# A two-layer gated cross-attention and feed-forward kernel: attention and FFN of a layer as one program with fixed, overlapping SBUF places

## The chip, the cores and the metric

One NeuronCore of a Trainium2 chip runs the whole kernel. The metric is the device time of one execution in microseconds (us). The kernel before takes 2742.32 us (median of 3 runs, 2741.12 to 2743.13).

## The reference, cut to what matters

Two layers work on `x`, 4096 rows (2 batches of 2048) of 512 values, against a context of 154 keys per batch. All is float32.

```
x = x + tanh(g_xattn[0]) * xattn0(layernorm(x), ctx)          # 16 heads of 32, softmax over 154 keys
x = x + tanh(g_ffn[0])   * (relu(layernorm(x) @ W1 + b1) @ W2 + b2)
x = x + tanh(g_xattn[1]) * xattn1(ctx, layernorm(x), mask)    # q, k, v are also layer-normalised
h = float2fix(layernorm(x) @ w1 + b1)                         # rounded to multiples of 1/256
h = float2fix(pwlin_gelu_basic(h))                            # 33-point piecewise linear GELU
x = x + tanh(g_ffn[1])   * float2fix(h @ w2 + b2)
```

W1 is 512 x 2048 and W2 is 2048 x 512.

## The kernel before

Every float32 product is made of three fp32r products, hi·hi, hi·lo and lo·hi (`hi_lo_matmul`, L56 is its matmul), so every weight and every left or right side is split into a hi part (ScalarE copies it as fp32r) and a lo part (the rest, by VectorE or GpSimd).

A layer is three programs, one after another, each with its own SBUF tiles, semaphores and an all-engine barrier at its end (`Named.end`): `context_phase` makes keys and values; `attention_phase` runs over 8 chunks of 512 rows; `ffn_phase` runs over the same 8 chunks. Between them the stream goes through DRAM. In the traces `l_ctx`, `l_att` and `l_ffn` tell them apart, for both layers alike.

Attention. The order of each engine is written out by hand. TensorE in chunk `it`: the transposes of the next chunk's rows (`xT_front`), the row maxima (`neg_front`, L836), the scores of the 26 tail keys, then per group of heads `scores_main` and `values_of`, with the next chunk's query products (`q_front`, four products of 12 matmuls) set between them as filler; `recips` (transposes of the reciprocal sums of the chunk before, L936), then `max_of` of the next chunk interleaved with `y_back` of the chunk before (48 matmuls of the output projection, L56 into `l_att_bank`). In the last chunk (7) nothing follows, so filler and `max_of` fall away. Then comes the drain: `sums_front(7)` (L919), `recips(7)`, `y_back(7)`. `y_back` has two PSUM banks; its rows are taken out by VectorE (L694), which needs the residual tile `xg` with its bias (`add_gate_bias`, GpSimd, L441), and `xg` is loaded only once the chunk before is stored (SP: `store`, then `load_residual`).

FFN. The hidden side is 16 tiles `m` of 128. Tile `u = 16*it + m` takes a first product (12 matmuls into `hid`), an activation, a split, and a second product (12 matmuls into the four accumulators `acc`) three tiles later (`LAG`). In layer 0 the activation is `relu_hi` on ScalarE and `relu_lo` on VectorE. In layer 1 it is a loop of three engines: VectorE `round_hidden` (L1277), ScalarE `gelu_ends` (three operations), GpSimd `slope_of` (L1136), VectorE `gelu` (L1284, L1289, L1293: three operations with two SBUF inputs each), ScalarE `rounded_hi` (L1202, L1207), VectorE `rounded_lo` (L1299). VectorE's order in tile `u` is `round_hidden(u)`, `rounded_lo(u-2)`, `gelu(u-1)`; ScalarE's is `gelu_ends(u)`, `rounded_hi(u-1)`.

The FFN weights stay in SBUF as hi and lo. They are brought in during chunk 0, tile by tile, through one staging buffer: two DMAs of 256 KB (SP: `weights(m)`, which waits until the lo parts of the tile before are made), two copies on ScalarE (`weights_hi`, L1213), two subtractions on GpSimd (`weights_lo`, L1124). `first_product` of chunk 0 waits for them tile by tile.

## Time and profile before

| what | value |
|---|---|
| median of 3 runs | 2742.32 us |
| the profiled execution, own time | 2744.99 us |
| its span, first to last instruction | 2743.2 us |
| TensorE matmul busy | 2480.5 us, 90% |
| VectorE, ScalarE, GpSimd busy | 53%, 39%, 18% |
| mean granted TensorE clock | 0.955 |
| DMA | 140.92 MB, mean 51 GB/s |
| layer 0 attention / FFN, TensorE's first to last matmul | 67.4 to 536.0 / 561.6 to 1282.3 us |
| layer 1 attention / FFN, TensorE's first to last matmul | 1364.4 to 1929.6 / 1950.5 to 2730.8 us |

The page cuts the span into 40 slices of 68.6 us; each digit is a busy share in tenths. A timeline row gives start, duration, engine, line, operation, output<-inputs, shape and count, and in square brackets the engine's idle time before it with its releaser. Rows of a group of instructions give busy us and the mean ns of one.

### The profile page before, as it was taken

The numbers are of one execution on the slowest core, as the hardware profiler recorded it, in microseconds if no ns is written. First come the engines' busy times: TensorE is split into PE (matmuls) and PEld (weight loads), VectorE is DVE, ScalarE is ACT, GpSimd is POOL, SyncE is SP. The second block draws the span as 40 slices with busy tenths as digits, with TensorE's granted clock in tenths as the row PEclk, the third lists the DMA queues.
The fourth block names the chain that finished last, engine by engine and source line by source line (L and its number), as shares of the span: only waits on it lengthen the run. The fifth ranks groups of instructions, "written<-read, shape, count | busy, mean of one in ns | idle before, by whom it ended". The sixth has DMA issues, their size and how long they took to land. (4 is left out here: it accounts for less than half of the span.)

```text
span 2743.2 us, 32089 instructions
## 1 busy us (share of the span) xinstructions
PE 2480.5 (90%) x12840; PEld 1860.6 (68%) x12864; DVE 1463.2 (53%) x2222; ACT 1078.3 (39%) x1734; POOL 505.4 (18%) x411
## 2 busy tenths in 40 slices
PE   4899999779999999996489999999579999999997
PEld 3557667458888888885355566665467788778776
DVE  4455565232222222211655665553488888888887
ACT  3233443243222222222223333332355666666564
POOL 1011211252000000001101111111462222222221
PEclk8799999889999999998699999999799999999999
DMA  3002111232001100102210111111321010101100
GB/s 129 31 16 81 59 47 47 86 114 81 16 31 46 46 27 20 47 31 75 95 41 28 59 59 59 59 44 62 100 82 53 16 46 32 47 16 34 44 16 31
DMA packets 87941, 140.92 MB, mean 51 GB/s; under 512 B 4848, under 2 KB 27760, under 8 KB 87792
## 3 DMA queue, kind: packets, MB, share of 16 engines
q1 hardware_dynamic: 87792, 138.87, 14.9%
q8 instruction: 102, 1.67, 0.2%
q14 instruction: 47, 0.39, 0.0%
HBM read 105.30 MB, written 33.55 MB: 51 GB/s over the span
## 5 line engine op out<-in xcount | busy, mean ns | idle before, releaser
L56 PE MATMUL l_ffn_hid<-l_ffn_xT_hi,l_ffn_w_hi 128*128 128x512 f32 x1024 | 406.0, 397 | 29.3 <-POOL l_ffn_w_lo L1124 29.3
L56 PE MATMUL l_ffn_acc<-l_ffn_w_hi,l_ffn_h_hi 128*128 128x512 f32 x1024 | 402.6, 393 | 18.1 <-DVE l_ffn_h_lo L1299 18.1
L56 PE MATMUL l_ffn_hid<-l_ffn_xT_hi,l_ffn_w_lo 128*128 128x512 f32 x1024 | 402.0, 393 | 0.0
L56 PE MATMUL l_ffn_hid<-l_ffn_xT_lo,l_ffn_w_hi 128*128 128x512 f32 x1024 | 401.9, 392 | 0.0
L56 PE MATMUL l_ffn_acc<-l_ffn_w_lo,l_ffn_h_hi 128*128 128x512 f32 x1024 | 399.5, 390 | 0.0
L56 PE MATMUL l_ffn_acc<-l_ffn_w_hi,l_ffn_h_lo 128*128 128x512 f32 x1024 | 399.2, 390 | 0.0
L1269 DVE TENSOR_TENSOR l_ffn_h_lo<-l_ffn_full,l_ffn_h_hi 128x512 fp32r<-128x512 f32 x128 | 88.6, 692 | 501.0 <-ACT l_ffn_h_hi L1181 501.0
L1136 POOL TENSOR_TENSOR l_ffn_at_next<-l_ffn_at_next,l_ffn_at_grid 128x512 f32<-128x512 f32 x128 | 187.5, 1465 | 491.7 <-ACT l_ffn_at_next L1197 491.6
L1176 ACT ACTIVATE l_ffn_full<-l_ffn_hid,l_ffn_b 128x512 f32<-128x512 f32 x128 | 88.2, 689 | 447.8 <-PE l_ffn_hid L56 447.8
L56 PEld LDWEIGHTS l_ffn_hid<-l_ffn_xT_hi,l_ffn_w_hi 128*128 128x128 f32 x1024 | 194.5, 190 | 76.0 <-POOL l_ffn_w_lo L1124 36.4
L56 PEld LDWEIGHTS l_ffn_acc<-l_ffn_w_hi,l_ffn_h_hi 128*128 128x128 f32 x1024 | 192.7, 188 | 65.0 <-DVE l_ffn_h_lo L1299 25.9
L56 PEld LDWEIGHTS l_ffn_hid<-l_ffn_xT_hi,l_ffn_w_lo 128*128 128x128 f32 x1024 | 194.2, 190 | 41.1
L56 PEld LDWEIGHTS l_ffn_hid<-l_ffn_xT_lo,l_ffn_w_hi 128*128 128x128 f32 x1024 | 194.9, 190 | 39.7
L667 DVE TENSOR_REDUCE l_att_maxes<-l_att_score 128x4 f32<-128x616 f32 x256 | 199.2, 797 | 41.1 <-PE l_att_score L826 39.2
L56 PEld LDWEIGHTS l_ffn_acc<-l_ffn_w_hi,l_ffn_h_lo 128*128 128x128 f32 x1024 | 192.8, 188 | 40.5
L56 PEld LDWEIGHTS l_ffn_acc<-l_ffn_w_lo,l_ffn_h_hi 128*128 128x128 f32 x1024 | 192.8, 188 | 39.1
L526 ACT ACTIVATE l_att_p_main<-l_att_score 128x512 f32<-128x512 f32 x256 | 132.2, 604 | 160.1 <-PE l_att_score L875 160.1
L826 PE MATMUL l_att_score<-l_k_bd,l_att_qT_hi 128*128 128x308 f32 x512 | 155.1, 385 | 11.7 <-DVE l_att_maxes L667 11.6
L1202 ACT ACTIVATE l_ffn_at_grid<-l_ffn_at_grid,l_ffn_grid_bias 128x512 f32<-128x512 f32 x128 | 92.7, 724 | 166.0 <-DVE l_ffn_at_grid L1293 166.0
L1293 DVE SCALAR_TENSOR_TENSOR l_ffn_at_grid<-l_ffn_at_next,l_ffn_at_grid 128x512 f32<-128x512 f32 x128 | 153.6, 1200 | 4.4
L488 ACT ACTIVATE l_att_xT_hi<-l_att_bank 128x512 fp32r<-128x512 f32 x64 | 36.7, 597 | 288.8 <-PE l_att_bank L780 288.8
L450 POOL COPY l_att_r_wide<-l_att_rs 128x512 f32<-128x512 f32 x64 | 37.4, 614 | 598.3 <-DVE l_att_rs L687 508.8
(191 smaller groups left out, 4309.3 us busy)
## 6 DMA issues: line engine op xcount, KB each, us to landing
stream<-l_att_xg SPq DMA_DIRECT2D x16, 1024.0 KB, 4.3
l_ffn_x_in<-stream SPq DMA_DIRECT2D x16, 1024.0 KB, 5.5
l_ffn_stage<-in_l_w SPq DMA_DIRECT2D x64, 256.0 KB, 2.8
l_ffn_xg<-stream SPq DMA_DIRECT2D x16, 1024.0 KB, 5.5
l_att_x_in<-in_x SPq DMA_DIRECT2D x8, 1024.0 KB, 6.5
l_att_xg<-in_x SPq DMA_DIRECT2D x8, 1024.0 KB, 5.3
stream<-l_ffn_xg SPq DMA_DIRECT2D x8, 1024.0 KB, 4.3
l_att_x_in<-stream SPq DMA_DIRECT2D x8, 1024.0 KB, 6.7
```

Of the source, the lines that this page charges most:

```text
L56: done = nc.tensor.matmul(out, lhs[a], rhs[b], start=first and n == 0, stop=last and n == len(passes) - 1)
L450: nc.gpsimd.tensor_copy(r_wide[:, t % RB, :, :].rearrange("p q (j d) -> p (q j) d", j=GH), rs[:, t, :, :].rearrange("p q j -> p (q j)").un ...
L488: nc.scalar.activation(xT[0][:, k, :], bank[k % 2][:, :], ACT.Copy)\
L526: nc.scalar.activation(p_main[:, t % 2, j, :], score[:, j, :], ACT.Exp)\
L667: nc.vector.tensor_reduce(to, heads, AX.X, ALU.max).then_inc(max_done, 1)
L826: done = nc.tensor.matmul(to, qT[it % QB][0][:, t, q * P:(q + 1) * P], keys.bd[:, b, t, 2 * a:2 * a + 2, :], start=not masked, stop=True)
L1136: nc.gpsimd.tensor_tensor(at_next[:, u % 2, :], at_next[:, u % 2, :], at_grid[:, u % AB, :], ALU.subtract).then_inc(slope, 1)
L1176: nc.scalar.activation(full[:, u % 2, :], hid[u % 2][:, :], ACT.Relu, bias=b1[:, u % MT:u % MT + 1]).then_inc(h_full, 1)
L1202: nc.scalar.activation(at_grid[:, u % AB, :], at_grid[:, u % AB, :], ACT.Identity, bias=grid_bias[:, 3:4]).then_inc(rounded, 1)
L1269: nc.vector.tensor_tensor(h[1][:, u % HB, :], full[:, u % 2, :], h[0][:, u % HB, :].bitcast(F32), ALU.subtract)\
L1293: nc.vector.scalar_tensor_tensor(at_grid[:, u % AB, :], at_next[:, s, :], -4.0, at_grid[:, u % AB, :], ALU.mult, ALU.add)\
```

## The change

`attention_phase` and `ffn_phase` become one `layer_phase`: one block, no barrier between them. All large tiles have fixed byte offsets (`Place.at`) in one arena, so that tiles with different lifetimes share bytes; the order that keeps them apart is in the waits. The FFN's PSUM tiles are attention's: `hid = bank`, `tr = [values, sums]`, and `score` is the accumulator.

- The rows of FFN chunk 0 are loaded, normalised and transposed as if they were attention chunk 8 (`load(8)`, `norm_stats(8)` in chunk 6, `xT_front(8)` in chunk 7).
- FFN weights: 16 places instead of one staging buffer, each raw tile landing where its lo part will stand; four tiles may be under way (`WB`). Tiles 0 and 1 are loaded once the last queries are made and split at the end of chunk 6; tiles 2 to 9 wait until the last probabilities are used (`p_used`), 10 to 15 until the last output product (`y_ps`).
- In chunk 7, first products 0 and 1 stand where `q_front` stood. `y_back(6)` follows `values_of(7, 3)`, with `sums_front(7)` after its first quarter; second products 0 and 1 stand between the halves of `recips(7)` and before `y_back(7)`. Tiles 2 to 15 follow, then chunks 1 to 7 as before.
- In chunk 0 weights are split four tiles ahead (`m + 4`) instead of one.
- One more small load (`b1`) at the layer's start; in layer 1 five memsets move there.
- The context phase's tiles lie in the same arena. Its work is the same.

```diff
+        def weights(m):
+            if m < 2:
+                sp.wait_ge(q_ps, KT * NCH)
+            elif m < 10:
+                sp.wait_ge(p_used, KT * NCH)
+            else:
+                sp.wait_ge(y_ps, QT * NCH)
+            if m >= WB:
+                sp.wait_ge(w_hi, 2 * (m - WB) + 1)
+            sp.dma_start(tw_raw[m][:, 0, :].rearrange("p (k c) -> p k c", k=KT), w1_v[m])\
+                .then_inc(w1_in[m % WB], 16)
...
             for it in range(NCH):
...
+                load(it + 2)
+                if norm and it + 2 < NCH:
+                    load_masks(it + 2)
+                if it == last - 1:
+                    weights(0)
+                    weights(1)
+                if it == last:
+                    for m in range(2, 2 + WB):
+                        weights(m)
+                    sp.dma_start(out_bias[:, :], w["b2_rows"]).then_inc(bias_in, 16)
                 if it:
                     store(it - 1)
                     load_residual(it)
+            for m in range(2 + WB, 10):
+                weights(m)
             store(last)
+            load_residual(NCH)
+            for m in range(10, MT):
+                weights(m)
...
         @block.gpsimd
...
+                if it == last - 1:
+                    weights_lo(0)
+                    weights_lo(1)
+            if norm:
+                slope_of(0)
+            widen(last, range(RB))
+            if norm:
+                slope_of(1)
+            weights_lo(2)
+            weights_lo(3)
+            widen(last, range(RB, KT))
+            add_bias(last, gate_bias)
+            for m in range(2, MT):
+                for mm in ((4, 5, 6) if m == 2 else (m + 4,)):
+                    if mm < MT:
+                        weights_lo(mm)
+                if norm:
+                    slope_of(m)
...
         @block.scalar
...
                 exps_tail(it)
+                if not norm:
+                    if more:
+                        q_front(it + 1, (0,))
+                    else:
+                        relu_hi(0)
                 exps_main(it, 0)
...
                 s_evict(it)
+                if it == last - 1:
+                    weights_hi(0)
+                    weights_hi(1)
+            if norm:
+                gelu_ends(0)
+                gelu_ends(1)
+            weights_hi(2)
+            weights_hi(3)
+            if norm:
+                rounded_hi(0)
+                rounded_hi(1)
             cT_back(last, range(KT))
+            for m in range(2, MT):
+                for mm in ((4, 5, 6) if m == 2 else (m + 4,)):
+                    if mm < MT:
+                        weights_hi(mm)
...
         @block.vector
...
+            xT_front(NCH)
+            recip_of(last - 1)
+            for u in range(2):
+                if norm:
+                    round_hidden(u)
+                else:
+                    relu_lo(u)
+            c_back(last - 1, (0, 1))
+            c_back(last - 1, (2, 3))
+            y_back(last - 1, 0)
             recip_of(last)
+            if norm:
+                gelu(0)
+            y_back(last - 1, 1)
+            if norm:
+                gelu(1)
+            y_back(last - 1, 2)
+            if norm:
+                rounded_lo(0)
+            y_back(last - 1, 3)
+            if norm:
+                rounded_lo(1)
+            c_back(last, (0, 1))
+            c_back(last, (2, 3))
             for q in range(QT):
                 y_back(last, q)
...
         @block.tensor
...
                 if more:
                     q_front(it + 1, (0,))
+                else:
+                    first_product(0)
                 scores_main(it, 0)
                 if more:
                     q_front(it + 1, (1,))
+                else:
+                    first_product(1)
                 scores_main(it, 1)
...
-            sums_front(last)
-            recips(last, range(KT))
+            values_of(last, 3)
+            for i in range(KT * QT):
+                y_back(last - 1, i)
+                if i == KT - 1:
+                    sums_front(last)
+            recips(last, (0, 1))
+            second_product(0)
+            recips(last, (2, 3))
+            second_product(1)
             for i in range(KT * QT):
                 y_back(last, i)
...
+            for u in range(2, MT * NCH):
+                f, m = u // MT, u % MT
+                first_product(u)
+                if f or m >= LAG + 2:
                     if m >= LAG:
+                        second_product(u - LAG)
+                    elif m < 2:
+                        second_product(MT * f - 2 + m)
```

## Rows read from the trace of the kernel before

**Rows 1.** The page's 40 slices: TensorE's busy share in tenths.
```profile
PE   4899999779999999996489999999579999999997
```

**Rows 2.** Stretches: us, busy us (instructions) of each engine, granted clock, DMA share, GB/s.
```profile
475.00:584.00 109.00, 72.39 (x399) 48.27 (x398) 33.67 (x47) 30.62 (x54) 33.89 (x26) 0.83 0.29 94
1866.00:2075.00 209.00, 156.85 (x746) 113.76 (x748) 122.21 (x136) 93.76 (x153) 89.53 (x69) 0.88 0.26 84
650.00:739.00 89.00, 89.00 (x402) 73.86 (x401) 20.96 (x37) 23.20 (x36) 5.96 (x3) 1.00 0.10 36
```

**Rows 3.** Timeline of TensorE, layer 0, last attention chunk to FFN's first tiles.
```profile
475.36 0.60 PE L836 MATMUL l_att_sums<-ident,l_att_maxes 128*128 128x128 f32 x4
503.06 0.51 PE L56 MATMUL l_att_bank<-l_wd_hi,l_att_xT_hi 128*128 128x512 f32 x1
...
514.18 0.96 PE L919 MATMUL l_att_sums<-l_att_gather,l_att_s_sb 128*128 128x16 f32 x8
516.47 1.21 PE L936 MATMUL l_att_bank<-ident,l_att_r_wide 128*128 128x128 f32 x8 [1.33 <-POOL l_att_r_wide L450]
...
522.48 0.80 PE L56 MATMUL l_att_bank<-l_wd_hi,l_att_xT_hi 128*128 128x512 f32 x1 [3.26 <-DVE l_att_xT_lo L681]
...
561.55 1.97 PE L1385 MATMUL l_ffn_tr<-ident,l_ffn_x_in 128*128 128x128 f32 x8 [25.57 <-DVE l_ffn_x_in L1256]
...
584.05 0.40 PE L56 MATMUL l_ffn_acc<-l_ffn_w_hi,l_ffn_h_hi 128*128 128x512 f32 x1
```

**Rows 4.** Timeline of TensorE, layer 0, between chunks: half of a chunk's transposes.
```profile
652.98 1.03 PE L1385 MATMUL l_ffn_tr<-ident,l_ffn_x_in 128*128 128x128 f32 x8
```

**Rows 5.** The chain that ended last: one product of 12 matmuls.
```profile
2266.36 2.73 PE l_ffn_hid L56 x12
```

**Rows 6.** The page's DMA issues: count, KB each, us from issue to landing.
```profile
stream<-l_att_xg SPq DMA_DIRECT2D x16, 1024.0 KB, 4.3
...
l_ffn_stage<-in_l_w SPq DMA_DIRECT2D x64, 256.0 KB, 2.8
...
l_att_xg<-in_x SPq DMA_DIRECT2D x8, 1024.0 KB, 5.3
```

**Rows 7.** Timeline of GpSimd, layer 0: chunk 7's residual bias; a weight tile's two splits.
```profile
524.76 4.61 POOL L441 TENSOR_TENSOR l_att_xg<-l_att_xg,l_att_gate_bias 128x2048 f32<-128x2048 f32 x1 [6.40 <-DMA l_att_xg<-in_x]
...
581.74 2.52 POOL L1124 TENSOR_TENSOR l_ffn_w_lo<-l_ffn_stage,l_ffn_w_hi 128x512 fp32r<-128x512 f32 x2 [2.18 <-ACT l_ffn_w_hi L1213]
```

**Rows 8.** Timeline of TensorE, layer 1, the same stretch.
```profile
1866.30 0.60 PE L836 MATMUL l_att_sums<-ident,l_att_maxes 128*128 128x128 f32 x4
...
1896.15 0.51 PE L56 MATMUL l_att_bank<-l_wd_hi,l_att_xT_hi 128*128 128x512 f32 x1
...
2074.55 0.39 PE L56 MATMUL l_ffn_hid<-l_ffn_xT_hi,l_ffn_w_hi 128*128 128x512 f32 x1
```

**Rows 9.** Waits from 1896 to 2075: us in total, times, longest.
```profile
PE l_ffn_hid L56 <- POOL l_ffn_w_lo L1124: 24.7, 12, 5.2
```

**Rows 10.** Groups of VectorE, 1984 to 2017, layer 1's chunk 0: busy us, mean ns.
```profile
L1284 DVE SCALAR_TENSOR_TENSOR l_ffn_full<-l_ffn_grid,l_ffn_full 128x512 f32<-128x512 f32 x5 | 8.9, 1786 | 0.0
L1293 DVE SCALAR_TENSOR_TENSOR l_ffn_at_grid<-l_ffn_at_next,l_ffn_at_grid 128x512 f32<-128x512 f32 x4 | 6.7, 1667 | 0.1
L1289 DVE SCALAR_TENSOR_TENSOR l_ffn_at_next<-l_ffn_full,l_ffn_at_next 128x512 f32<-128x512 f32 x4 | 6.6, 1640 | 0.1
```

**Rows 11.** Groups of GpSimd, the same stretch.
```profile
L1124 POOL TENSOR_TENSOR l_ffn_w_lo<-l_ffn_stage,l_ffn_w_hi 128x512 fp32r<-128x512 f32 x10 | 14.9, 1511 | 13.3 <-ACT l_ffn_w_hi L1213 13.3
L1136 POOL TENSOR_TENSOR l_ffn_at_next<-l_ffn_at_next,l_ffn_at_grid 128x512 f32<-128x512 f32 x4 | 6.9, 1737 | 0.0
```

**Rows 12.** Groups of VectorE, 2125 to 2160, a later chunk, no weights being split.
```profile
L1289 DVE SCALAR_TENSOR_TENSOR l_ffn_at_next<-l_ffn_full,l_ffn_at_next 128x512 f32<-128x512 f32 x7 | 4.8, 692 | 0.2
L1299 DVE SCALAR_TENSOR_TENSOR l_ffn_h_lo<-l_ffn_at_grid,l_ffn_h_hi 128x512 fp32r<-128x512 f32 x7 | 4.8, 689 | 4.4 <-ACT l_ffn_h_hi L1207 4.4
```

**Rows 13.** Timeline of ScalarE, layer 1's chunk 0: the first of `rounded_hi`'s two operations.
```profile
1990.66 0.73 ACT L1202 ACTIVATE l_ffn_at_grid<-l_ffn_at_grid,l_ffn_grid_bias 128x512 f32<-128x512 f32 x1 [2.82 <-DVE l_ffn_at_grid L1293]
```

1079 lines of the change are left out of this document (497 added, 582 removed).

## The prediction

> **What bounds the kernel now.** I read the page's slices first [rows 1]: TensorE is at nine tenths or more nearly everywhere, so the kernel is bound by matmuls except in four dips, at the two starts of a context phase and at the two seams between attention and FFN (slices 8 and 9, and 29 and 30). The change leaves the context phases' work alone, so only the seams matter. The table of stretches gives their size [rows 2]: from 475 to 584 us TensorE is busy 72.4 of 109 us, from 1866 to 2075 us 156.9 of 209, both at a granted clock under 0.9, while an ordinary FFN stretch has 89.0 of 89 at 1.00. The timeline then names the waits. In layer 0 the seam's large one is 25.57 us before the first FFN transpose [rows 3]: store of the last chunk, barrier, load, statistics, normalisation. Small ones stand before it (1.33 and 3.26 us in the drain). In layer 1 the weights go on limiting: 12 waits for GpSimd's lo parts, 24.7 us in all [rows 9].
>
> **How I count.** The new order of work is fixed, so I date the same piece of remaining work before and after. Prices: a product of 12 matmuls 2.73 us [rows 5], half of a chunk's transposes 1.03 [rows 4], `y_back` 514.18 - 503.06 = 11.1, `sums_front` 0.96, half of `recips` at most 1.2 [rows 3]. Durations are of the profiled execution (2744.99 us of its own, span 2743.2); it is 0.1% over the median, so I subtract the difference from the median.
>
> **Layer 0.** Before, chunk 7 starts at 475.36 and at 584.05 four of the 32 products of FFN chunk 0 are done [rows 3]. After:
> - Chunk 7 up to its last values took 503.06 - 475.36 = 27.7 us. Added: two halves of transposes (2.1) and first products 0 and 1 (5.5). So `y_back(6)` starts at 475.4 + 35.3 = 510.7. It and `sums_front` end at 522.7.
> - `recips`, second 0, `recips`, second 1: 2.3 + 5.5 = 7.8, to 530.5. The 3.26 us that TensorE waited for the split of the last values [rows 3] now lie behind second 1 (2.73), which leaves 0.5: 531.0.
> - `y_back(7)` has two banks, so after half of it (5.6, at 536.6) it waits for VectorE to take out row one, which waits for the residual: `y_back(6)` out at about 523.5, store 4.3, load 5.3 [rows 6], bias 4.61 [rows 7], one output row 0.75 (an estimate from VectorE's 0.69 for such an operation [rows 12]): 538.5. Then 5.6 more: 544.1. This route was under the wait for `y_back(7)` before as well; SP now has weight loads 2 to 5 queued in front of that store, but they are released 12 us earlier and take some 4 us to issue.
> - At 544.1, again four of 32 products are done. The gain is 584.05 - 544.1 = 40.0. The clock in chunk 7 was not full (0.83 over the stretch [rows 2]), and the first products fill short waits for the exponentials; both can give back 0 to 4. I take 41.
> - After that TensorE stays fed: a tile's two lo parts cost GpSimd 2.52 in this layer [rows 7] against 5.46 of products, and weights are split four tiles ahead. Tiles 10 to 15 are loaded behind the residual of chunk 0, at about 544 + 0.8 + 4.3 = 549, and landed by 555; ScalarE wants tile 10 at tile 6, about 557. Two us of room, and if it is gone ScalarE's copy delays `relu_hi(6)`, which has the lag of three tiles as cover.
>
> **Layer 1.** Before, chunk 7 starts at 1866.30 and the first product of FFN chunk 1 at 2074.55 [rows 8]. After:
> - Values end at 1866.3 + 29.85 [rows 8] + 2.1 + 5.5 = 1903.7; `y_back(6)` and `sums_front` would end at 1915.7. But VectorE now has both `gelu` calls between the output rows of `y_back(6)`. The first can't end before ScalarE has emptied chunk 7, switched its table and made the ends, and GpSimd the slope, about 1910; each `gelu` beside GpSimd's splitting costs 1.79 + 1.64 + 1.67 = 5.1 [rows 10]. So output row 2 leaves at about 1920, and with it `recips`. Then 1.2 + 2.7 + 1.2 + 2.7 plus 1.5 for the rows between: `y_back(7)` from about 1929, its second half from about 1936 (the residual's route again: 1921.5 + 4.3 + 5.3 + 4.6 + 0.75), end about 1941. The old drain ended at 1929.6 with four products fewer.
> - Tiles 3 to 11 are split and activated together. VectorE's loop per tile: it ends `gelu`; `round_hidden` runs beside ScalarE's two operations of `rounded_hi` (2 x 0.73 [rows 13]); `rounded_lo` 0.6 on from there; then `gelu`. GpSimd gets its next split 0.6 us after `rounded_hi`, which is just when `gelu` starts, and its work, 2 x 1.51 + 1.74 = 4.8 us [rows 11], covers `gelu` nearly whole. So a tile takes 1.45 + 0.6 + 5.1 = 7.2 us, hardly less than the 7.34 it took in chunk 0 before: more weight buffers don't help here, since the collision stays. Without a split the three operations take 0.69 each [rows 12] and TensorE's 5.46 bounds.
> - `gelu(2)` ends about 11 us after first product 2 starts, at 1952; eight tiles of 7.2 bring 2009.6. From there TensorE has 2.05 + six products + two transposes = 20.5 to go: FFN chunk 1 starts at 2030. Gain 2074.5 - 2030 = 44.
> - Statistics and normalisation for FFN chunk 1 fall into this stretch before and after; I cost them at nothing extra, since GpSimd's split runs alone meanwhile and a later collision is saved.
>
> Here a page bears on it. The trace shows both sides slowed when they meet: the three VectorE operations 5.1 instead of 2.1 us, GpSimd's 1.51 and 1.74 each [rows 10 to 12]. The Trainium skill, page "SBUF — State Buffer", section "Who interferes with whom", says that VectorE with two SBUF inputs and a reading GpSimd instruction exclude each other for the whole instruction. By that rule, strictly alternating, the loop would be longer; the rows are what the sum uses.
>
> **Costed at nothing.** The `b1` load (about half a microsecond of SP) sits before the residual load; TensorE's start hangs on the first rows' statistics. The early load and normalisation of chunk 8 take VectorE time in chunk 6, which every earlier chunk also had. Splits of tiles 0 and 1 lie on ScalarE and GpSimd while both idle at the end of chunk 6. `relu_hi(0)` and `(1)` delay the exponentials of chunk 7 by under 0.5 us, beside `scores_main`. Bounds: 0 to 2 us each way.
>
> **Sum.** 41 + 44 = 85; 2742.3 - 85 = **2657 us**.
>
> **Rivals.**
> - *Layer 1's tiles run at TensorE's pace* (0.12). GpSimd has 4.8 us of work in a 7.2 us tile; if its phase slips so that the split meets `round_hidden` and the wait instead of `gelu`, eight tiles gain 7.2 - 5.46 each, 14 us: 2643. Against it: the release times above lock the phase.
> - *The early tiles don't fit into the drain* (0.17). Attention's drain had only some 5 us of idle TensorE for 10.9 us of products, and now GpSimd's queue holds `widen` of the second half behind the splits of tiles 2 and 3, which wait for loads released only at the end of the values. My count from release: landing 2.8 to 5.3 [rows 6], copies 2, splits 6, `widen` 1.2: 12 to 14.5, wanted at 16. Eight loads at once may land as slowly as two of 1 MB, 10.6; then each seam is 3 to 6 us longer: 2663 to 2669. The overlap then gives nothing and all the gain is the boundary's 25 and 21 us and the weights' pace.
> - *Full exclusion of GpSimd and VectorE* (0.04). If the two took strict turns, VectorE's 3 x 0.69 [rows 12] and GpSimd's three operations at 1.26 each, as when alone [rows 7], would need 5.9 in place of 5.1: 0.8 over eight tiles and the drain's two `gelu`, 8 us: 2665. Against it: the same meeting took 5.1 here. The section of the Trainium skill named above would have it so.
> - *Slower than before* (0.03). The same collision gets into the steady tiles of layer 1: the 112 tiles of chunks 1 to 7 have only 5.46 of TensorE cover over a VectorE loop of 2.05 + 2.1 + one slowed operation (1.0). If `slope_of` met all three, a tile would take 7.2, 1.74 more: 195 us, 2852. It turns the sign from 0.76 us per tile. Against it: chunks 1 to 7 keep their order, and a change of PSUM names and places is no reason for another phase.
> - *No net change* (0.01): half of the above.
> - The forecast's own case (0.63) spans 2647 to 2666 by the terms above.
>
> **Range and chances.** 2640 to 2672 holds the forecast, the first two rivals and the exclusion in their larger part. Faster by over 0.2% (5.5 us, about what a measurement of this kernel can tell) 0.96, within 0.2% 0.01, slower 0.03.
>
> **What would show it.** No TensorE wait over 4 us between chunk 7 and FFN chunk 1; in layer 0 the third first product some 69 us after chunk 7's start and no waits for lo parts; in layer 1 VectorE's three `gelu` operations at 1.6 to 1.8 us until the splits end, a tile rhythm near 7.2, and chunk 1 some 164 us after chunk 7's start instead of 208; later FFN chunks as long as before. A `recips` wait on `widen`, or a rhythm near 5.5, or longer chunks 1 to 7 would prove me wrong in the named way.

## The result, and the profile after

The changed kernel takes 2677.3 us (median of four runs, 2675.9 to 2679.4) against 2742.7: ratio 0.9763, interval 0.9746 to 0.9780. That is 65.4 us won, where I had forecast 85; the time lies 5 us above my range. The profiled execution took 2679.4 us with a span of 2677.5, so its spans can be compared with those of before directly.

The stretches of the changed kernel that answer [rows 2] (us, busy us and instructions of PE, PEld, DVE, ACT, POOL, granted clock, DMA share, GB/s):

```profile
475.00:584.00 109.00, 105.55 (x578) 78.29 (x576) 37.62 (x53) 49.80 (x88) 51.10 (x40) 0.98 0.42 138
1836.00:2008.00 172.00, 150.69 (x748) 109.68 (x747) 112.26 (x123) 91.06 (x149) 83.11 (x56) 0.95 0.28 91
650.00:739.00 89.00, 89.00 (x395) 72.58 (x395) 20.52 (x37) 22.26 (x35) 6.24 (x3) 1.00 0.11 36
```

The first line is the seam of layer 0: TensorE was busy 72.4 us of these 109 before and is now busy 105.6. The second is layer 1's seam, from the start of chunk 7 to FFN chunk 1: 748 matmuls in 172 us, before 746 in 209. The third is the line that I had not looked for. It is an ordinary FFN stretch of layer 0, TensorE busy all the time and at full clock in both kernels, and yet 395 matmuls fit into it where 402 did before [rows 2].

TensorE's timeline of the changed kernel, layer 0 (start, duration, line, out<-in; in brackets the wait before it), which answers [rows 3] and [rows 4]; the last line is layer 1's first product, and its bracket gives the end of layer 0, 1273.26 - 21.16 = 1252.10:

```profile
474.63 0.60 PE L1216 MATMUL l_lay_sums<-ident,l_at_maxes 128*128 128x128 f32 x4
...
505.39 0.50 PE L66 MATMUL l_lay_bank<-l_at_wd_hi,l_at_xT_hi 128*128 128x512 f32 x1
...
518.85 0.48 PE L66 MATMUL l_lay_score<-l_at_tw_hi,l_at_h_hi 128*128 128x512 f32 x1
...
525.30 0.39 PE L66 MATMUL l_lay_bank<-l_at_wd_hi,l_at_xT_hi 128*128 128x512 f32 x1
...
533.80 0.50 PE L66 MATMUL l_lay_bank<-l_at_wd_hi,l_at_xT_hi 128*128 128x512 f32 x1 [2.89 <-DVE l_at_xg L949]
...
541.02 0.39 PE L66 MATMUL l_lay_bank<-l_at_xTf_hi,l_at_tw_hi 128*128 128x512 f32 x1
...
604.82 0.60 PE L1160 MATMUL l_lay_values<-ident,l_at_x_in 128*128 128x128 f32 x4
...
695.26 0.60 PE L1160 MATMUL l_lay_values<-ident,l_at_x_in 128*128 128x128 f32 x4
...
1273.26 0.79 PE L66 MATMUL l_ctx_ps<-l_at_ctx_wk_hi,l_at_ctx_ctx_hi 128*128 128x512 f32 x1 [21.16 <-DVE l_at_ctx_wk_lo L251]
```

`y_back(6)` starts at 505.39, second product 0 at 518.85, `y_back(7)` at 525.30, and its second half at 533.80 after the wait for the residual. That half, 24 matmuls, takes not 5.5 but 7.2 us, until first product 2 starts at 541.02, because the granted clock fell behind the wait. Layer 1 shows the same. The stretches of the first 12 matmuls behind the residual's wait, in layer 0 and in layer 1:

```profile
533.80:538.25 4.45, 4.45 (x12) 3.52 (x13) 0.60 (x1) 0.00 (x0) 4.45 (x5) 0.62 0.02 6
1904.41:1909.69 5.28, 5.28 (x12) 4.17 (x13) 0.60 (x1) 0.00 (x0) 5.28 (x5) 0.50 0.01 4
```

These 12 matmuls take 4.45 and 5.28 us at a granted clock of 0.62 and 0.50, where they take 2.72 at 1.00; 0.50 is the lower of the clock's two levels, 1.2 GHz. So the wait of 2.89 us was followed by a loss of 1.7 us more, and the one of 3.46 us by 2.9 us more (the 12 matmuls after those shown took 3.08).

At 541.02 four of the 32 products of FFN chunk 0 are done, as at 584.05 before. Counted from chunk 7's start that is 66.4 us against 108.7: 42.3 won, and 0.7 came before it. But layer 0 ends at 1252.10, before at 1302.95 - 20.68 = 1282.27 (the same row of the kernel before): only 30.2 us are left. In between, 12.9 us were given back, 1.2 of them in chunk 0 and 11.6 from there on. The two lines of 604.82 and 695.26 show how: they are the same transposes of successive chunks, 90.44 us apart, where before the distance was 741.82 - 652.98 = 88.84 us:

```profile
741.82 1.03 PE L1385 MATMUL l_ffn_tr<-ident,l_ffn_x_in 128*128 128x128 f32 x8
```

Every chunk is 1.6 us longer, in nearly every one of its products (only the two of tile 0 and the second one of tile 1 still take 2.72 to 2.74 us), and no wait is recorded.

The same timeline in layer 1, which answers [rows 8]:

```profile
1836.25 0.60 PE L1216 MATMUL l_lay_sums<-ident,l_at_maxes 128*128 128x128 f32 x4
...
1904.41 0.80 PE L66 MATMUL l_lay_bank<-l_at_wd_hi,l_at_xT_hi 128*128 128x512 f32 x1 [3.46 <-DVE l_at_xg L949]
...
1912.77 0.39 PE L66 MATMUL l_lay_bank<-l_at_xTf_hi,l_at_tw_hi 128*128 128x512 f32 x1
...
1926.22 0.50 PE L66 MATMUL l_lay_score<-l_at_tw_hi,l_at_h_hi 128*128 128x512 f32 x1 [2.29 <-DVE l_at_h_lo L984]
...
1933.55 0.50 PE L66 MATMUL l_lay_score<-l_at_tw_hi,l_at_h_hi 128*128 128x512 f32 x1
...
1940.91 0.50 PE L66 MATMUL l_lay_score<-l_at_tw_hi,l_at_h_hi 128*128 128x512 f32 x1 [1.58 <-DVE l_at_h_lo L984]
...
1995.07 0.60 PE L1160 MATMUL l_lay_values<-ident,l_at_x_in 128*128 128x128 f32 x4
...
2003.50 0.63 PE L1160 MATMUL l_lay_values<-ident,l_at_x_in 128*128 128x128 f32 x4 [1.79 <-DVE l_at_xTf_lo L875]
...
2007.28 0.39 PE L66 MATMUL l_lay_bank<-l_at_xTf_hi,l_at_tw_hi 128*128 128x512 f32 x1
```

FFN chunk 1 starts 2007.28 - 1836.25 = 171.0 us after chunk 7, before 208.25 [rows 8]: 37.2 won, forecast 44. The second products come every 7.35 us (1926.22, 1933.55, 1940.91).

Together: 0.7 + 42.3 - 12.9 in layer 0, - 0.5 at the boundary (21.16 against 20.68), + 0.4 in layer 1's attention, + 37.2 in its seam, - 1.6 behind it (a chunk takes 92.79 against 92.64): 65.7 us before rounding. So two questions stood open: what makes the same matmuls slower, and whether the 7.35-us rhythm is the collision of VectorE and GpSimd that I had forecast.

### The profile page after: what moved, and what is told of

It is laid out like the page before. It is cut to its first block, busy times and chain, and to the rows that moved or that the text cites. A ratio compares the mean times of both kernels' runs of the same rounds, so it can differ in the third digit from the quotient of the medians.

```text
span 2677.5 us, 32104 instructions
## 1 busy us (share of the span) xinstructions
PE 2487.4 (93%) x12864; PEld 1854.4 (69%) x12864; DVE 1461.5 (55%) x2222; ACT 1075.8 (40%) x1734; POOL 508.8 (19%) x407
## 4 chain that ended last, share of the span: by engine, by line
PE 37%; DVE 9%; ACT 2%; issue 2%; DMA 1%; POOL 0%; ACTq 0%; DVEq 0%
PE l_lay_bank L66 16%; PE l_lay_score L66 10%; DVE l_at_at_grid L978 2%; DVE l_at_at_next L974 1%; DVE l_at_full L969 1%; PE l_lay_score L1204 1%; PE l_lay_values L1265 1%; PE l_lay_score L1206 1%; PE l_lay_score L1246 1%; PE l_lay_score L1252 1%; PE l_lay_sums L1277 1%; PE l_lay_values L1269 1%; DVE l_at_h_lo L984 1%; PE l_lay_bank L1160 1%; DVE l_at_xTf_lo L875 1%
## 5 line engine op out<-in xcount | busy, mean ns | idle before, releaser
L66 PE MATMUL l_lay_score<-l_at_tw_hi,l_at_h_hi 128*128 128x512 f32 x1024 | 409.3, 400 | 28.1 <-DVE l_at_h_lo L984 28.1
L66 PE MATMUL l_lay_score<-l_at_tw_hi,l_at_h_lo 128*128 128x512 f32 x1024 | 404.9, 395 | 0.0
L66 PE MATMUL l_lay_score<-l_at_tw_lo,l_at_h_hi 128*128 128x512 f32 x1024 | 404.3, 395 | 0.0
L66 PE MATMUL l_lay_bank<-l_at_xTf_hi,l_at_tw_hi 128*128 128x512 f32 x1024 | 403.9, 394 | 0.0
L66 PE MATMUL l_lay_bank<-l_at_xTf_lo,l_at_tw_hi 128*128 128x512 f32 x1024 | 402.4, 393 | 0.0
L66 PE MATMUL l_lay_bank<-l_at_xTf_hi,l_at_tw_lo 128*128 128x512 f32 x1024 | 402.3, 393 | 0.0
L66 PEld LDWEIGHTS l_lay_score<-l_at_tw_hi,l_at_h_hi 128*128 128x128 f32 x1024 | 193.4, 189 | 80.8 <-DVE l_at_h_lo L984 37.9
L66 PEld LDWEIGHTS l_lay_score<-l_at_tw_hi,l_at_h_lo 128*128 128x128 f32 x1024 | 193.4, 189 | 45.5
L66 PEld LDWEIGHTS l_lay_score<-l_at_tw_lo,l_at_h_hi 128*128 128x128 f32 x1024 | 193.8, 189 | 43.4
L922 DVE TENSOR_REDUCE l_at_maxes<-l_lay_score 128x4 f32<-128x616 f32 x256 | 198.9, 797 | 40.4 <-PE l_lay_score L1206 37.9
L1206 PE MATMUL l_lay_score<-l_at_k_bd,l_at_qT_hi 128*128 128x308 f32 x512 | 155.5, 386 | 11.7 <-DVE l_at_maxes L922 11.6
```

Of the source, the lines that this page charges most:

```text
L66: done = nc.tensor.matmul(out, lhs[a], rhs[b], start=first and n == 0, stop=last and n == len(passes) - 1)
L922: nc.vector.tensor_reduce(to, heads, AX.X, ALU.max).then_inc(max_done, 1)
L1206: done = nc.tensor.matmul(to, qT_of(it)[0][:, t, q * P:(q + 1) * P], keys.bd[:, b, t, 2 * a:2 * a + 2, :], start=not norm, stop=True)
```

## Why the same matmuls take longer

Three things differ for TensorE in an FFN chunk: the PSUM banks (accumulators now in `score`, banks 2 to 5, the hidden tile in `bank`, 0 and 1), the places in SBUF, and what the other engines do at those places.

**Banks.**

```
-        bank = [n.ps(f"bank{i}", [P, 512]) for i in range(2)]
         score = n.ps("score", [P, GH, 512])
+        bank = [n.ps(f"bank{i}", [P, 512]) for i in range(2)]
```

> The changed kernel with only the order of its PSUM tensors exchanged, so that the feed-forward accumulators lie in banks 0 to 3 and the hidden tile in banks 4 and 5, as in the kernel before. Theory of banks: the product of 12 matmuls falls from 2.77 to 2.72 us, a layer 0 chunk from 90.45 to 88.84 us, and the time from 2677.3 to about 2663 us. Theory of places in SBUF, or of what shares them: nothing changes, 2677 us within 2 us.

Measured 2677.6 us (ratio to before 0.9768, 0.9753 to 0.9782), and the chunks keep 90.45 us. The banks have no part in it.

**TensorE alone.** A kernel of nothing but these matmuls, with the places as the variable. The sections are divided by one transpose group each:

> This is no attention kernel: it leaves the whole computation out and only repeats, on TensorE with every other engine silent, the matmuls of one feed-forward chunk (16 tiles, 192 matmuls of the first product and 192 of the second), eight times over with other places. Section 1: places and PSUM banks of the changed kernel. 2: its places with the banks of the kernel before (accumulators 0 to 3, hidden 4 and 5). 3: places and banks of before. 4: places of before with the banks of the changed kernel. 5: weight tiles of the changed kernel, inputs and hidden places of before. 6: the reverse of 5. 7: tiles one after another in 8192 bytes each, inputs and hidden places of before. 8: as 1 with every place rounded down to a multiple of 2048 bytes. Theory of places in SBUF (some addresses of weights and moving data disturb each other): sections 3 and 4 take 2.72 us per product of 12 matmuls, 1 and 2 take 2.72 to 2.80 depending on the tile, as in the changed kernel, 87 against 89 us per section, and sections 5 to 8 say which place it is. Theory of banks: 2 and 3 are fast, 1 and 4 slow. Theory of another engine (PE's reads disturbed by what VectorE and ScalarE do at the changed places): all eight sections take 2.72 us per product.

TensorE's timeline, the rows that divide the sections:

```profile
118.85 0.60 PE L83 MATMUL bank<-ident 128*128 128x128 f32 x4
...
207.94 0.60 PE L83 MATMUL bank<-ident 128*128 128x128 f32 x4
...
295.47 0.60 PE L83 MATMUL bank<-ident 128*128 128x128 f32 x4
...
382.97 0.60 PE L83 MATMUL bank<-ident 128*128 128x128 f32 x4
...
472.22 0.60 PE L83 MATMUL bank<-ident 128*128 128x128 f32 x4
...
559.95 0.60 PE L83 MATMUL bank<-ident 128*128 128x128 f32 x4
...
647.45 0.60 PE L83 MATMUL bank<-ident 128*128 128x128 f32 x4
...
734.96 0.27 PE L93 MATMUL bank<-ident 128*128 128x128 f32 x1
```

Read as differences, they give section 2 (changed kernel's places) 89.09 us, 3 and 4 (places of before, either banks) 87.53 and 87.50, 5 (only the weight tiles as in the changed kernel) 89.25, 6 (only inputs and hidden tiles so) 87.73, 7 (tiles one after another in 8192 bytes) 87.50, and 8 (the changed kernel's places rounded down to 2048 bytes) 87.51. Section 1 contains the start from rest and is left out. So no other engine is needed, it is the weights' addresses, and it is not that a tile's high and low parts now lie side by side (section 7): rounding the same places is the whole cure. Where do they lie? The constants of the kernel put tiles 0 and 1 at a multiple of 2048, tiles 2 to 9 at 960 bytes past one, 10 to 13 at 1664 and 14 and 15 at 1920; the inputs and hidden tiles 0 and 1 stand at a multiple, hidden tiles 2 and 3 at 960. The single products point at the offset between the two operands of a matmul. Tile m uses hidden tile m mod 4, and the second products of tiles 2 and 6, weights and hidden tile both at 960, take 2.73 us in sections 1 and 2 and in the changed kernel; those of tiles 4, 5 and 8 to 10, whose two operands stand differently, take 2.79 to 2.80. Tiles 3 and 7, both operands at 960 as well, take 2.77 and 2.76, which that alone doesn't explain.

**Which offset counts.**

> As m1_tensor_alone (no attention kernel, the whole computation left out, TensorE alone, one feed-forward chunk's 384 matmuls per section), the places those of the kernel before, which took 87.5 us, with parts of them moved by some bytes. Sections: 1 nothing moved; the weights moved by 64 (2), 128 (3), 256 (4), 512 (5), 1024 (6), 960 (7), 1664 (8) and 1920 bytes (9); weights, inputs and hidden tiles all moved by 960 (10), by 240 (11), by 48 (12); only the inputs by 960 (13); only the hidden tiles by 960 (14); the weights by 32 (15). Theory of relative alignment (the weights' address against that of the inputs and hidden tiles, modulo 2048, decides): section 7 about 89.2 us, 10 to 12 stay at 87.5, 13 and 14 lie between. Theory of absolute alignment: 7 and 10 both about 89.2 us. Theory of neighbourhood (far or near places, whatever their alignment): all sections 87.5 us within 0.2.

Length of each section, as the difference of two such dividing rows (three of those rows below: sections 3 and 4 lie between them, moved by 128 and by 256 bytes):

```profile
207.51 0.60 PE L82 MATMUL bank<-ident 128*128 128x128 f32 x4
...
297.46 0.60 PE L82 MATMUL bank<-ident 128*128 128x128 f32 x4
...
384.99 0.60 PE L82 MATMUL bank<-ident 128*128 128x128 f32 x4
```

| moved | bytes: us per section |
|---|---|
| weights only | 32: 90.02, 64: 89.35, 128: 89.95, 256: 87.53, 512: 87.50, 1024: 87.51, 960: 89.59, 1664: 89.95, 1920: 89.53 |
| inputs only, hidden only | 960: 89.03, 87.93 |
| all together | 960: 87.49, 48: 88.76, 240: 89.18 |

All offsets of the weights that are multiples of 256 bytes cost nothing, the others that I tried cost 1.9 to 2.5 us in 87.5. Moving everything by 960 costs nothing, moving the weights alone by 960 costs 2.1, so the offset of one operand against the other counts. My theory was incomplete, though: moved by 48 or 240 together, where it expected 87.5, they take 88.8 and 89.2, so the common start has a part too (48 and 240 are no multiples of 64, 960 is). Why that is stays open, and so does whether 256 would be the step from another common start.

**In the full kernels.** The places moved by 64 to 128 bytes, as a short diff:

```
-BD_AT = EARLY + 22208
+BD_AT = EARLY + 22272
-LATE = MIDDLE + 51904
+LATE = MIDDLE + 51968
-        negT = at("negT", MIDDLE + 3 * T2 + 704, [P, CHUNK], F32R)
+        negT = at("negT", MIDDLE + 3 * T2 + 768, [P, CHUNK], F32R)
...
```

> The changed kernel with its fixed places moved by 64 to 128 bytes so that every place whose data TensorE reads lies at a multiple of 256 bytes from the first one (until now the weight tiles 2 to 9 lay 192 bytes off, 10 to 15 128 bytes off). Theory of relative alignment: the product of 12 matmuls takes 2.72 us, a layer 0 chunk 88.8 us instead of 90.45, so 14 us are won in layer 0 and 1 to 2 in layer 1, in all 2662 us; if the attention's matmuls gain too (its inputs lay off their weights in both kernels) up to 10 us more, 2652. Rival (in the full kernel the other engines' accesses slow TensorE, the alignment counts only when it runs alone): 2677 us within 3 us.

Measured 2658.7 to 2666.1 us in three runs (ratio 0.9703, 0.9687 to 0.9719); the fourth, the profiled one, took 5027 us for a reason that stays open, and nothing is read from it. So the same kernel once more:

> The same kernel as e6_places_at_256, whose profiled execution was disturbed: 2659 to 2664 us, a layer 0 chunk of 88.8 us, and from this profile where the gain lies: 11 us in the seven later chunks of layer 0, some 3 us in its first chunk and the last attention chunk, 1 us in layer 1's chunks.

Measured 2659.9 us (2658.6 to 2661.2), ratio to before 0.9699, 0.9683 to 0.9716: 17.4 us under the changed kernel. Its profile, the stretch of layer 0 again and two successive chunks' transposes:

```profile
650.00:739.00 89.00, 89.00 (x402) 73.93 (x401) 20.98 (x37) 23.23 (x36) 5.97 (x3) 1.00 0.10 36
```
```profile
604.01 0.60 PE L1160 MATMUL l_lay_values<-ident,l_at_x_in 128*128 128x128 f32 x4
...
692.85 0.60 PE L1160 MATMUL l_lay_values<-ident,l_at_x_in 128*128 128x128 f32 x4
```

402 matmuls again, and 88.84 us to the hundredth. Of the 19.7 us between the two spans the later chunks of layer 0 give 11.6, as expected. My division of the rest was off. Layer 0's seam and first FFN chunk together lost 0.1: the chunk's products gave 1.2, but the residual's wait grew to 3.25 us, and the 24 matmuls behind it took 8.2 us instead of 7.2, the granted clock being low for longer. The attention of both layers gave 2.3 us, layer 1's seam 4.8 and what follows 1.1. Of the 4.8 us 4.7 lie in the drain: the residual's wait was 1.23 us instead of 3.46, and the clock stayed at 1.00 behind it. No run shows that the places did that. What they surely gave is the pace of the products.

The reverse, in the kernel before:

```
         w2 = [n.sb(f"w2_{x}", [P, MT, D], F32R) for x in ("hi", "lo")]
+        n.sb("pad", [P, 16])
```

> The kernel before with one edit: an unused 64-byte tensor between the feed-forward weights and what follows them (stage, inputs, hidden tiles), so that these lie 64 bytes off relative to the weights. Theory of relative alignment: the layer 0 chunks go from 88.84 to about 90.6 us, eight of them, 14 us, and layer 1, where VectorE sets the pace, loses 0 to 2 us: 2756 to 2758 us. Rival (what slows the changed kernel is something that only it has): 2742.5 us, within 2 us.

Measured 2762.1 us, ratio 1.0071 (1.0050 to 1.0091), so 19.8 us lost by 64 unused bytes, more than the 14 to 16 expected (16.7 between the spans of the two profiled executions): a layer 0 chunk takes 90.97 us, 2.13 more, and a layer 1 chunk about 93.2, 0.5 more. The distance of two successive chunks' transposes:

```profile
739.14 1.03 PE L1386 MATMUL l_ffn_tr<-ident,l_ffn_x_in 128*128 128x128 f32 x8
...
830.11 1.03 PE L1386 MATMUL l_ffn_tr<-ident,l_ffn_x_in 128*128 128x128 f32 x8
```

The cause is settled from both sides: the 12.9 us of layer 0 went into the addresses of the fixed places, and so did 1.1 of the 1.6 us behind layer 1's seam.

## The rhythm of layer 1's first tiles

VectorE and GpSimd of the changed kernel in one tile:

```profile
1933.41 1.80 DVE L969 SCALAR_TENSOR_TENSOR l_at_full<-l_at_grid,l_at_full 128x512 f32<-128x512 f32 x1
1935.24 1.67 DVE L974 SCALAR_TENSOR_TENSOR l_at_at_next<-l_at_full,l_at_at_next 128x512 f32<-128x512 f32 x1
1936.94 1.67 DVE L978 SCALAR_TENSOR_TENSOR l_at_at_grid<-l_at_at_next,l_at_at_grid 128x512 f32<-128x512 f32 x1
```
```profile
1933.37 2.99 POOL L574 TENSOR_TENSOR l_at_tw_lo<-l_at_tw_raw,l_at_tw_hi 128x512 fp32r<-128x512 f32 x2 [2.67 <-ACT l_at_tw_hi L715]
1936.32 1.75 POOL L580 TENSOR_TENSOR l_at_at_next<-l_at_at_next,l_at_at_grid 128x512 f32<-128x512 f32 x1
```

GpSimd's three operations (1933.37 to 1938.07) cover VectorE's `gelu` (1933.41 to 1938.61) nearly whole, as the prediction had it [rows 10, 11]. The ends of the instructions show more: the two engines take turns. GpSimd's second split ends at 1936.36 and VectorE's second operation 0.55 us later; GpSimd's slope ends 1.16 us after that, at 1938.07, and VectorE's third operation 0.54 us after the slope. Alone such instructions take 0.69 us on VectorE and 1.29 on GpSimd, so all but 0.14 us of each is spent while the other one stands. It holds throughout: of the 88 VectorE operations that a split or a slope of GpSimd stretches in layer 1, 87 end 0.54 to 0.56 us after one of GpSimd's.

To show that this cover is the cause, the split was taken away (this kernel leaves the low part of those weights out and reads their high part in its place, so its output is wrong and only its time is of use):

```
+                    w = 8 if norm and m >= 4 else D
-                    nc.gpsimd.tensor_tensor(tw_lo[m][:, i, :], tw_raw[m][:, i, :],
-                                            tw_hi[m][:, i, :].bitcast(F32), ALU.subtract)\
+                    nc.gpsimd.tensor_tensor(tw_lo[m][:, i, 0:w], tw_raw[m][:, i, 0:w],
+                                            tw_hi[m][:, i, 0:w].bitcast(F32), ALU.subtract)\
```

> The changed kernel; in layer 1, from tile 4 on, GpSimd's two subtractions per weight tile are made of 8 columns only and TensorE reads the high part twice instead (the low part of the weights is left out there). Theory of my prediction (VectorE and GpSimd slow each other down where they meet, 5.1 us for three operations of the gelu): the rhythm of layer 1's first tiles falls from 7.35 us to between 5.5 and 5.9 us, eight or nine tiles from tile 3 to 11, so feed-forward chunk 1 starts 12 to 16 us earlier and the time is 2661 to 2665 us. Rival (the rhythm of 7.35 us is ScalarE's or the weights' transfer): the rhythm stays above 7 us and the time within 3 us of 2677.

Measured 2657.1 us, ratio 0.9690 (0.9671 to 0.9710). That is 20.2 us, more than the 12 to 16 expected. In the trace FFN chunk 0's transposes come 138.6 us after chunk 7's instead of 159.3, and the three operations have their own length:

```profile
1935.53 0.70 DVE L970 SCALAR_TENSOR_TENSOR l_at_full<-l_at_grid,l_at_full 128x512 f32<-128x512 f32 x1
1936.27 0.69 DVE L975 SCALAR_TENSOR_TENSOR l_at_at_next<-l_at_full,l_at_at_next 128x512 f32<-128x512 f32 x1
1936.99 0.69 DVE L979 SCALAR_TENSOR_TENSOR l_at_at_grid<-l_at_at_next,l_at_at_grid 128x512 f32<-128x512 f32 x1
```

TensorE then takes 5.6 us per tile without a gap. Eight tiles at 1.78 us less make 14.2. Of the rest 4.7 lie ahead of them: the second product of tile 2 comes 85.3 us after chunk 7's start instead of 90.0. Of these 1.9 are the collision again, since `gelu(2)` takes 2.9 us instead of 4.8 with the splits of tiles 4 to 6 gone from beside it. The other 2.8 lie in the drain, where the waits are nearly the same (2.77 and 3.39 us) but the granted clock fell less behind them; that the edit did this isn't shown. So 16 us are the collision's, as expected. The last 1.8 are about what statistics and normalisation cost the changed kernel (below).

**Who should do the split?** If GpSimd's split costs VectorE 1.8 us a tile, VectorE could do the same work itself, 2 x 0.69:

```
+            def weights_lo(m):
+                for i in range(2):
+                    dve.wait_ge(w_hi, 2 * m + i + 1)
+                    dve.wait_ge(w_lo, 2 * m + i)
+                    nc.vector.tensor_tensor(tw_lo[m][:, i, :], tw_raw[m][:, i, :],
...
                     round_hidden(u)
+                    if 3 <= u and u + 4 < MT:
+                        weights_lo(u + 4)
```

> The changed kernel; in layer 1 the low parts of weight tiles 4 to 15 are subtracted by VectorE (0.69 us for 512 columns, two for each tile), tiles 4 to 6 in its gaps in the last output projection, the others one per tile of chunk 0, instead of by GpSimd (1.26 to 1.48 us each). Theory (GpSimd's splits cost VectorE 1.8 us per tile by collision): VectorE then needs about 4.2 us of its own work and 1.4 us of splits, the rhythm falls from 7.35 to between 5.9 and 6.5 us, and 8 to 14 us are won: 2663 to 2669 us. Rival (VectorE is the bound either way, and 1.4 us more of work costs what the collision cost): 2675 to 2679 us.

Measured 2675.8 us (2674.6 to 2675.9), ratio 0.9755 (0.9740 to 0.9769): 1.5 us, no difference that these intervals can tell. The rival's time came out, but not by its reason. The profiled executions say a little more: layer 1's seam is 5.1 us shorter, but 4.6 of that lie in the drain (a residual wait of 1.69 us, the clock at 1.00 behind it), and 1.8 us were lost before chunk 7 of layer 0, where the edit does nothing. The timeline of VectorE:

```profile
1930.95 1.49 DVE L877 TENSOR_TENSOR l_at_tw_lo<-l_at_tw_raw,l_at_tw_hi 128x512 fp32r<-128x512 f32 x2 [1.40 <-ACT l_at_tw_hi L717]
...
1935.38 0.69 DVE L988 SCALAR_TENSOR_TENSOR l_at_at_grid<-l_at_at_next,l_at_at_grid 128x512 f32<-128x512 f32 x1
...
1938.14 1.49 DVE L877 TENSOR_TENSOR l_at_tw_lo<-l_at_tw_raw,l_at_tw_hi 128x512 fp32r<-128x512 f32 x2 [1.41 <-ACT l_at_tw_hi L717]
```

VectorE isn't busy all the time: it waits 1.41 us in each tile for ScalarE's high part. Where I had put the split it closed a loop: the end of `gelu`, ScalarE's two roundings (1.47) and two high parts (1.14), the split (1.49), the low part and the next `gelu`, 7.19 us. The collision was gone and a new wait had its place. The same split behind `gelu`, where its input has long been ready, was tried on top of the other two repairs, and these come first.

## The route of the residual, and the gap that the products fill

**The residual in four parts.** The store of chunk 6, the load of chunk 7's residual into the same place and the bias, by rows of 128 for this chunk alone:

```
+            def parts():
+                for q in range(QT):
+                    sp.wait_ge(y_done, QT * (last - 1) + q + 1)
+                    sp.dma_start(mid_v[last - 1][:, q, :], xg[:, q, :]).then_inc(part_out[q], 16)
+                    if q:
+                        part_load(q - 1)
+                part_load(last_q)
```

> The changed kernel; for the last attention chunk the store of the chunk before it, the load of the residual into the same place and GpSimd's addition of the bias go in four parts of 128 rows each instead of one. Theory (TensorE's waits of 2.89 us in layer 0 and 3.46 us in layer 1 before the third group of the last output projection are this route, in which the load is only issued when the store has landed): both waits go and the time falls by 4 to 6.4 us, to 2671 to 2673 us. Rival (the route is hidden behind something that comes next, GpSimd's low parts in layer 1 above all): only layer 0's 2.9 us or nothing is won, 2674 to 2678 us.

Measured 2673.0 us (2672.1 to 2673.2), ratio 0.9747 (0.9731 to 0.9764). That is 4.3 us below the changed kernel; the intervals of the two ratios overlap, so the trace has to carry it. There both waits before the second half of `y_back(7)` are gone, and a new, shorter one stands before its first half, for the low parts of the context:

```profile
526.63 0.50 PE L66 MATMUL l_lay_bank<-l_at_wd_hi,l_at_xT_hi 128*128 128x512 f32 x1 [0.70 <-DVE l_at_xT_lo L965]
...
1894.03 0.50 PE L66 MATMUL l_lay_bank<-l_at_wd_hi,l_at_xT_hi 128*128 128x512 f32 x1 [1.56 <-DVE l_at_xT_lo L965]
```

The second half itself takes 5.44 us in both layers at a granted clock of 1.00, instead of 7.2 and 8.4. From chunk 7's transposes to those in FFN chunk 0 it takes 3.8 us less in either layer. So the waits of 2.89 and 3.46 us were on the path, in layer 1 as well, and with them the slow clock behind them. The two sides differ by 7.3 us in the profiled executions and by 4.3 in the medians: the changed kernel's profiled execution was the slowest of its four, this one the fastest of its four.

**The products behind the drain.**

```
             recips(last, (0, 1))
-            second_product(0)
             recips(last, (2, 3))
-            second_product(1)
             for i in range(KT * QT):
                 y_back(last, i)
+            second_product(0)
+            second_product(1)
```

> The changed kernel with the second products of tiles 0 and 1 moved from between the transposes of the reciprocals to behind the last output projection. Theory (they fill a gap whose length VectorE, ScalarE and GpSimd set): the output projection of the last chunk starts when it did, and the products then cost 2 x 2.72 = 5.4 us behind it, in layer 0 in full, in layer 1 less, since there VectorE sets the rhythm of the tiles behind: 2677.3 + 5.4 to + 10.9, taken 2684. Rival (the products in the gap held up the projection by themselves): the projection starts up to 5.4 us earlier and the time stays at 2677.

Measured 2687.5 us, ratio 0.9805 (0.9789 to 0.9821): 10.2 us more than the changed kernel. TensorE's timeline:

```profile
476.13 0.60 PE L1216 MATMUL l_lay_sums<-ident,l_at_maxes 128*128 128x128 f32 x4
...
525.39 0.50 PE L66 MATMUL l_lay_bank<-l_at_wd_hi,l_at_xT_hi 128*128 128x512 f32 x1 [3.25 <-DVE l_at_xT_lo L936]
...
535.48 0.50 PE L66 MATMUL l_lay_bank<-l_at_wd_hi,l_at_xT_hi 128*128 128x512 f32 x1 [2.75 <-DVE l_at_xg L949]
```

Without the products the wait of 3.25 us for the context's low parts is back, the very wait of 3.26 us of [rows 3], and the second half of `y_back(7)` starts 59.35 us after chunk 7, where the changed kernel has it at 59.17. In layer 0 the two products in the gap are free and cost their full 5.6 us behind it. In layer 1 the second half starts 2.0 us earlier without them (66.1 against 68.2 us) and isn't slowed by the clock, so first product 2 starts only 0.7 us later (77.2 against 76.5 us after chunk 7's start), and that is about what layer 1 costs in the end. The rest of the 10.2 us is scatter: this execution had reached chunk 7 of layer 0 1.5 us later, and the changed kernel's median lies 2.1 us below its profiled execution.

## The repairs together

> Parts of the residual (e5), places at 256 bytes (e6) and the split on VectorE (e9) together. If the three are independent: 2677.3 - 4.3 - 15 - 8 to 14, so 2644 to 2650 us, less if the attention gains by its places too. If VectorE's rhythm hides what TensorE wins in layer 1: 2 us more than that.

Measured 2655.2 us (2654.1 to 2655.3), ratio 0.9680 (0.9663 to 0.9696). The expected 2644 to 2650 counted 8 to 14 us for the split, which alone gave 1.5; 2677.3 - 4.3 - 17.4 - 1.5 would be 2654.1, so the parts add up.

```
-                    if 3 <= u and u + 4 < MT:
-                        weights_lo(u + 4)
...
                         gelu(u - 1)
+                    if 3 <= u and u + 4 < MT:
+                        weights_lo(u + 4)
```

> As e10_all_three, with VectorE's split of weight tile u + 4 moved behind the gelu of tile u - 1. In e9 and e10 it stood ahead of the low part of tile u - 2 and waited 1.41 us for ScalarE in every tile, which closed a loop of 7.19 us (ScalarE's two roundings 1.47 us, its two high parts 1.14 us, then VectorE's split and gelu). Theory of the loop: VectorE's own work remains, 0.74 + 0.69 + 0.69 + 1.67 + 0.69 + 1.49 = 5.97 us per tile, so the rhythm is about 6.0 us, eight tiles win 1.2 us each, and the time is 2644 to 2648 us. Rival (work on VectorE, wherever it stands, costs the same): 2655 us within 2 us.

Measured 2644.1 us (2643.0 to 2646.3), ratio 0.9643 (0.9628 to 0.9657). The timeline of VectorE:

```profile
1935.20 0.69 DVE L1017 SCALAR_TENSOR_TENSOR l_at_at_grid<-l_at_at_next,l_at_at_grid 128x512 f32<-128x512 f32 x1
1935.81 2.58 DVE L906 TENSOR_TENSOR l_at_tw_lo<-l_at_tw_raw,l_at_tw_hi 128x512 fp32r<-128x512 f32 x2
...
1941.02 0.69 DVE L1017 SCALAR_TENSOR_TENSOR l_at_at_grid<-l_at_at_next,l_at_at_grid 128x512 f32<-128x512 f32 x1
```

One edit of place, 11 us: the loop theory holds. A tile takes VectorE 5.82 us (1935.20 to 1941.02), with no wait in it. It isn't quite as I summed it: the split now takes 2.58 us instead of 1.49, since GpSimd's `slope_of` meets it there and no longer the middle operation of `gelu`, which is back at 0.69; the slope ends at 1937.05, and the first half of the split 0.55 us behind it. This version beats both kernels, the changed one by 33 us and the one before by 98.

## Why the prediction was right and wrong, step by step

- **Layer 0's seam, forecast 40 to 41: 42.3.** The chain of dates holds in its order and in the wait that ends last; that the sum fits so well is partly luck. `y_back(6)` came at 30.8 us after chunk 7's start, forecast 35.3: the added transposes and first products cost 3.1 us and not 7.6, since they filled waits for the exponentials and the clock was no longer low in this stretch (0.98 against 0.83). I had allowed 0 to 4 for this and taken 1. Against that the residual's wait was 2.89 us, forecast 1.9, and the half of `y_back(7)` behind it, priced at 5.6, took 7.2 because the granted clock had fallen. I had no term for a clock that falls behind a wait.
- **"After that TensorE stays fed" in layer 0: fed, but 12.9 us slower.** Here the prediction failed. The price of a product, 2.73 us [rows 5], was carried over to a kernel whose operands have other addresses, where most products take 2.75 to 2.80. I costed the change of places at nothing; the one word on it, in the rival "Slower", is that it is no reason for another phase of VectorE. "Later FFN chunks as long as before" stood as a sign to watch, and it is the sign that showed the failure. The kernel's own offsets, 22208 and 51904, are no multiples of 256 bytes, and all weight tiles but two stand behind them. With its share of layer 1 the term is 12.9 + 1.6 = 14.5 us; without it 65.4 + 14.5 = 79.9 us would have been won, 5 short of the forecast, and the time, 2662.8 us, would lie in the range. The changed kernel with repaired places measured 2659.9.
- **Layer 1's drain, forecast end 74.7 us after chunk 7's start: 76.5.** Right in its order, with the residual's wait as its last (3.46 us), and the second half of `y_back(7)` even started 1.5 us earlier than forecast (68.2 against 69.7). It then took 8.4 us and not 5.6, the granted clock having fallen to 0.50, so the drain ended 1.8 us late. That `recips` waits for output rows which stand behind VectorE's `gelu` calls was right too (2.77 us).
- **Tiles 3 to 11 at 7.2 us: 7.33 to 7.37,** but for the two below, and only up to tile 10, where the splits end. Right in mechanism and nearly in size; the loop is 5.2 of `gelu`, 1.5 of ScalarE and 0.6 of `rounded_lo`. Removing the split proved it, and refuted the rival of TensorE's pace (2643), whose phase never slipped.
- **Statistics and normalisation at nothing: 1.5 us.** The tiles that hold them took VectorE 8.2 and 8.05 us (ends of `gelu` at 1953.33 and 1961.52, 1976.24 and 1984.29). Beside that `gelu(2)` ended 2.0 us late, nearly all of it the drain's 1.8, the rhythm cost 0.15 a tile, and behind the last of these tiles there were 23.0 us to go, not 20.5, 1.79 of them the wait at 2003.50. These make 2.0 + 2.8 (the 1.5 and eight times 0.15) + 2.5 = 7.3 us, which is why layer 1's seam gave 37 and not 44. This shortfall and the price of the products make up the miss; without either of them the time would have been in the range.
- **Rival "the early tiles don't fit".** Its route did slow: the 256-KB weight loads land in 5.4 us (median) instead of 2.8 [rows 6]. But `recips` waited 0.50 us in layer 0 and 2.77 in layer 1, both times for an output row and not for `widen`; the drain had room. With the two products moved behind the drain layer 0's seam grew by their full 5.6 us, so there the gap had held them.
- **Full exclusion of GpSimd and VectorE (2665).** Its mechanism was right and its price wrong. The ends of the instructions show strict turns, 0.55 us of VectorE's and 1.15 of GpSimd's at a time. I had priced a turn by the whole duration of each instruction when alone, 3 x 0.69 + 3 x 1.26 = 5.9 us; three turns of each are 3 x 0.55 + 3 x 1.15 = 5.1, which is what the rows of before had and the sum used. So there was no slower case left to come, and "against it: the same meeting took 5.1 here" was no argument against turns. The Trainium skill, page "SBUF — State Buffer", section "Who interferes with whom", has the two exclude each other; the trace agrees, but for 0.14 us of each instruction that the other's turn covers.
- **Slower.** The steady tiles of layer 1 kept their phase, 92.79 against 92.64 us a chunk.
- **The range.** It took in the unknown waits of the seams, but none of the price of the FFN's products, 2 x 8 x 32 x 2.73 = 1,398 us that I took over from the old profile. A doubt of 0.5% on that price (7 us) would have covered the result, though the measured 1.8% of a layer 0 chunk is more.

## What to carry to other kernels

When a change gives tensors fixed places by hand, treat the offsets as part of the timing: keep every operand that TensorE reads at the same remainder of 256 bytes (no run with the weights moved by a multiple of 256 lost anything, but common shifts by 48 and 240 bytes did, so the remainder alone is no guarantee), and compare the number of matmuls in a fully busy stretch of the same length before and after, since this loss shows no wait, no lower clock and no idle engine. Price a wait of TensorE together with the clock behind it: here 2.89 us of waiting cost 4.6. When one engine's work is slowed by a neighbour, moving the neighbour's work to it helps only if the new place has its input ready; look for the loop that the new wait closes before counting the saved microseconds.

## What the runs showed of the hardware that I had not expected

- TensorE's pace in back-to-back matmuls of 128x512 float32r depends on the byte offset between the places of the two operands: 226.7 ns from start to start at equal remainders of 256 (2.72 us for 12), about 231 ns with the changed kernel's places, with every engine but TensorE silent as well. Sections with weights 32 to 1920 bytes off, at no multiple of 256, took 1.9 to 2.5 us more in 87.5. A common shift by 48 or 240 bytes cost 1.3 and 1.7 us, one by 960 nothing.
- The loss belongs to single tiles and repeats: in the changed kernel the second product of tile 2 takes 2.73 us, of tile 7 2.76 and of tile 8 2.80 in each of the chunks 1 to 7 of both layers, though VectorE and ScalarE do quite different work in the two.
- TensorE's granted clock fell behind its waits in the drain: 12 matmuls took 4.45 us (0.62) behind a wait of 2.89 us and 5.28 us (0.50, 1.2 GHz) behind one of 3.46, against 2.72 at 1.00. With the waits removed the same half of `y_back(7)` ran at 1.00 in both layers.
- VectorE's operations with two SBUF inputs and GpSimd's `tensor_tensor` of two SBUF tiles take turns, instruction by instruction: VectorE's of 128x512 ends 0.54 to 0.56 us after the GpSimd instruction beside it, and GpSimd's ends 1.15 us after VectorE's (0.69 and 1.29 us alone). Whichever of VectorE's operations lies there pays, up to 1.8 us instead of 0.69: in the last version the split paid (2.58 instead of 1.49 for two) and the `gelu` went free.
